# Attention: the V products of a head pair in three groups of four key blocks in place of six groups of two

## The reference, cut to what matters

```
q, k, v = (xn @ w + b)         16 heads of 64, rotary on q and k
scores  = q k^T / 8, masked    1024 x 1024 per head
attn    = softmax(scores)
ctx     = attn @ v
out     = ctx @ o_w + o_b + xn
```

## Time and profile before

| | us |
|---|---|
| runs of the kernel | 2549.84, 2547.35, 2551.39; median 2549.84 |
| the profiled execution's own time | 2540.03 |
| its span (first to last instruction) | 2538.2 |
| granted TensorE clock, mean over the span | 0.923 of full speed |

### The profile page before, as it was taken

How to read it: one execution, slowest core, us unless ns; L and a number is a source line. 1 busy time by engine, 2 the same in 40 slices (tenths; PEclk the granted TensorE clock), 3 DMA queues, 4 the chain that set the end, 5 groups by cost and what they waited for, 6 DMA issues and landing times.

```text
span 2538.2 us, 41109 instructions
## 1 busy us (share of the span) xinstructions
PE 2080.7 (82%) x10326; PEld 1351.3 (53%) x10326; DVE 1746.0 (69%) x3011; ACT 1431.7 (56%) x2785; POOL 902.7 (36%) x733
## 2 busy tenths in 40 slices
PE   3749999879675999987966699997896579999699
PEld 1236666647324666655732466664562256666466
DVE  3957676759485767667947667675794766767588
ACT  3516666647542766655744366664674356666366
POOL 1544242223154433313315534240332453333122
PEclk9879999989896999998979799999897879999889
DMA  2000000001000000001100000000100000000011
GB/s 59 1 25 6 9 8 0 1 25 40 11 0 25 10 5 8 0 1 32 35 10 0 25 10 5 8 0 9 29 29 9 17 13 5 9 4 0 9 35 31
DMA packets 36211, 35.48 MB, mean 14 GB/s; under 512 B 3993, under 2 KB 30977, under 8 KB 36097
## 3 DMA queue, kind: packets, MB, share of 16 engines
q1 hardware_dynamic: 36096, 34.14, 4.6%
HBM read 32.03 MB, written 2.10 MB: 13 GB/s over the span
## 4 chain that ended last, share of the span: by engine, by line
PE 54%; DVE 21%; issue 11%; ACT 8%; POOL 4%; DVEq 1%; ACTq 1%; DMA 0%; SPq 0%; POOLq 0%
PE ps L1314 10%; PE ps L1153 8%; PE ps L1155 6%; PE ps L1154 6%; DVE state L900 5%; PE ps L1303 5%; PE ps L1293 3%; ACT probs L665 3%; DVE turned L948 3%; PE ps L1329 3%; PE ps L1294 3%; PE ps L1421 2%; PE ps L1181 2%; ACT probsT L677 2%; DVE q_split L963 2%
## 5 line engine op out<-in xcount | busy, mean ns | idle before, releaser
L677 ACT ACTIVATE probsT<-ps 128x512 f32<-128x512 f32 (+3 forms) x768 | 351.1, 498 | 446.3 <-PE ps L1303 445.0
L516 POOL TENSOR_TENSOR roped<-turned 128x512 f32<-128x512 f32 x128 | 192.8, 1507 | 663.1 <-DVE turned L948 663.1
L665 ACT ACTIVATE probs<-ps,least 128x640 f32<-128x640 f32 (+7 forms) x512 | 383.3, 749 | 59.5 <-DVE least L973 53.5
L1293 PE MATMUL ps<-k_high,q_split 128*128 128x512 f32 (+3 forms) x768 | 310.0, 404 | 65.4 <-POOL k_low L527 38.7
L1303 PE MATMUL ps<-ident,probs 128*128 128x128 f32 x2304 | 349.9, 279 | 10.3 <-ACT probsT L677 10.1
L1303 PEld LDWEIGHTS ps<-ident,probs 128*128 128x128 f32 x2304 | 261.5, 142 | 133.8 <-issue 94.3
L1314 PE MATMUL ps<-probsT,vals 128*64 128x512 f32 (+3 forms) x1536 | 293.0, 506 | 5.2 <-ACT probsT L677 5.2
L973 DVE CUSTOM_DVE_ANT_0 ps<-ps,row_masks 128x128 f32<-128x128 f32 (+3 forms) x256 | 127.6, 498 | 222.7 <-PE ps L1294 220.2
L980 DVE TENSOR_REDUCE least<-ps 128x1 f32<-128x640 f32 (+3 forms) x256 | 262.3, 1024 | 8.8
L1294 PE MATMUL ps<-k_low,q_split 128*128 128x512 f32 (+3 forms) x768 | 260.6, 352 | 0.0
L725 ACT ACTIVATE hid<-ps,cols 128x512 f32<-128x512 f32 x256 | 176.5, 690 | 103.1 <-PE ps L1155 76.6
(11 more groups left out here) (213 smaller groups left out, 4135.6 us busy)
## 6 DMA issues: line engine op xcount, KB each, us to landing
w<-in_w SPq DMA_DIRECT2D x128, 128.0 KB, 2.0
w_pair<-in_w_pairs SPq DMA_DIRECT2D x36, 256.0 KB, 2.7
xin<-in_x SPq DMA_DIRECT2D x5, 512.0 KB, 3.9
out<-acc SPq DMA_DIRECT2D x4, 512.0 KB, 3.6
pos<-in_c_pos SPq DMA_DIRECT2D x1, 512.0 KB, 4.9
v_w<-in_v_w SPq DMA_DIRECT2D x1, 512.0 KB
o_w<-in_o_w SPq DMA_DIRECT2D x1, 512.0 KB
v_b<-in_v_b SPq DMA_DIRECT2D x1, 512.0 KB
```

What stands on the lines that cost most here:

```text
L516: pool.tensor_tensor(roped[:, k, c * HALF:(c + 1) * HALF], turned[:, 0, g % 2, :], turned[:, 1, g % 2, :], ALU.add).then_inc(roped_ready, 1)
L665: act.activation(probs[:, t % 2, 0:width(t)], banks(2 * (t % 2))[:, 0:width(t)], ACT.Exp, bias=least[:, t:t + 1], scale=-1.0, accum_out=ro ...
L677: act.activation(dst, ps[:, T_BANK + g % 2, 0:k1 - k0], ACT.Copy).then_inc(t_taken, 1)
L1293: pe.matmul(o, q, k_high[par][h][:, k0:k1], start=True, stop=False)
```

## The change

Three groups replace six. Half 1 of the pair before is made in slots 2 (key blocks 0 to 3) and 5 (key blocks 4 to 7); half 0 of this pair is made in slot 11 (key blocks 0 to 3). The products, their operands and the order among them are the same. No wait is added or taken away, and no other engine's code is touched.

```
-                        if t in (1, 3, 5, 7) and not first:
-                            weigh_values(n - 1, 1 - par, 1, (t - 1, t))
-                        if t in (10, 11):
-                            weigh_values(n, par, 0, (2 * t - 20, 2 * t - 19))
+                        if t in (2, 5) and not first:
+                            weigh_values(n - 1, 1 - par, 1, tuple(range(TPH)) if t == 2 else tuple(range(TPH, TILES)))
+                        if t == 11:
+                            weigh_values(n, par, 0, tuple(range(TPH)))
```

## The result

| | before | after |
|---|---|---|
| median of 4 runs each on the same chip, us | 2548.6 | 2610.17 |
| ratio to before, 95% interval | 1 | 1.024 (1.0223 to 1.0258) |
| the profiled execution's own time, us | 2540.03 | 2611.41 |
| its span, us | 2538.2 | 2609.6 |
| granted TensorE clock, mean | 0.923 | 0.915 |

The account below looks back on a forecast made before the run. PE was taken to bound slots 1 to 6, DVE slots 7 to 10, then PE and ACT alternating. 1.09 + 1.38 = 2.47 us, times 24 = 59.3, plus 4.8, on 2549.8 gave 2614 us; range 2580 to 2634.

Parts of the forecast that it names:

- The joins: Merging groups of V products saves 0.14 us per join; merged groups take 3.58, 2.31 and 2.31 us.
- the rival by which the joins pay (2537): All V products: 88 joins save 0.14 us each, 12 us in all, and nothing waits; 2537 us, chance 0.07.
- Slots 1 to 6: Loop pair until project(7): bare slots shrink less than filled ones grow, +1.09 us in sum.
- fixed floor: Slots without V products: none shorter than about 1.92 us, as project must wait until DVE's `turned` empties the one bank.
- Slots 10 and 11: Loop pair: values(1) starts 0.13 us earlier, V products behind it take 1.51 more; transposes come 1.38 us later.
- slot 7 gives nothing back: Slot 7 is 0.80 us lighter on PE, but DVE sets that stretch, so +1.09 us stays.
- a rival for all pairs behind the two waits (2729): Slot 11: the clock falls behind waits of 1.32 and 1.5 us, +115 us more, 2729 us; chance 0.05.
- a clock below 1.00 in a loop pair: Changed profile, any loop pair: a granted clock under 1.00 would show the working wrong.
- the rival of 2581: DVE's stretch: its copy escapes POOL, 0.43 us for 2.27, so a pair costs only +1.09; 2581 us, chance 0.13.
- Pair 0: First pair of each batch: slot 11 +1.51, slot 10 -0.3, so +1.2 us, times 4 = +4.8 us.
- Pair 7: Last pair of each batch: shift hidden behind a 2.42 us wait, 0 us, bounds -0.5 and +1.5 each.
- my likeliest range: Whole kernel: 2.0 to 3.0 us per loop pair with the ends of pairs 0 and 7, 2596 to 2630 us.

Follow-up runs that it names:

- the experiment in slot 10: Half 0 as one group in slot 10 behind the output product, half 1 as before, against the kernel before: 2537.81 us, 0.9966.
- Half 1 alone: Only half 1 moved to slots 2 and 5, half 0 as before, against the kernel before: 2595.27 us, 1.0192; again 2593.39 us.
- Half 0 alone: Only half 0 moved to slot 11 as one group, half 1 as before, against the kernel before: 2580.55 us, 1.0142.
- half 0 ahead: Half 0 as one group in slot 10 ahead of the output product, half 1 as before, against the kernel before: 2523.99 us, 0.9907.

## Why the prediction was right

The order of the steps is that of the working.

- **The joins.** 3.58, 2.31 and 2.31 us, to the hundredth. But a join is worth more than its own 0.14: with what stands beside it, 0.23 in the window of the experiment in slot 10 and 0.33 in the period. In the changed kernel PE has 0.41 us less to do in a pair, and waits for more than that, so the rival by which the joins pay (2537) falls. That the 0.14 comes from the change between 64 and 128 columns is not shown: no run has a join without it.
- **Slots 1 to 6.** +1.03 measured, +1.09 said. Slot 1 1.92 (said 1.92), slot 2 4.99 (5.05), slot 3 1.70 (1.80), slot 4 2.02 (1.91), slots 5 and 6 5.84 (5.85). A slot without V products lasts from project's start until the bank is free, as said, and PE waits 0.55, 0.28 and 0.36 us at the ends of slots 1, 3 and 4. But 1.92 us is no fixed floor: `turned` starts 1.11, 0.89 and 1.21 us behind project in these slots and runs 0.75, which with the 0.06 gives the 1.92, 1.70 and 2.02. Slot 3 lies 0.1 below my lower bound for it, and slot 4 above my value by as much; the two cancel. Half 1 alone shows it apart (+1.0).
- **Slots 10 and 11.** From project(7) to values(1) 12.26 us against 333.47 - 321.08 = 12.39: -0.13 as said. From values(1) to the transposes 3.39 against 1.78: +1.61, said +1.51; the 0.1 is `values` itself, 1.08 behind a wait where it was 0.98. Half 0 alone gives +1.52 for the period. The kernel with half 0 ahead shows from the other side that the loss is the place behind the wait: the same group there gains.
- **What I overlooked.** Slot 7's lighter work goes into slot 10's wait: 2.06 us in place of 1.32. I had said that slot 7 gives nothing back, and did not draw the wait that follows from it. In itself it costs nothing, since DVE sets that stretch; but it is the wait behind which the clock fell.
- **The clock.** Here the working was wrong and got away with it. I gave the lower clock 0.05, as a rival for all pairs behind the two waits (2729), and named a clock below 1.00 in a loop pair as a sign that I am wrong. That sign came in 13 of 24 pairs, behind the first wait and not the second. In 12 of them it slowed only slot 10's products, and the new wait in slot 11 took that up; in one it reached slot 11 and cost 2.0 us. Nothing in my working had this, so the small cost is luck. At 1.6 us each, as with half 1 alone, the 13 would have added 19 us more: 2629, still in the range.
- **DVE's copy.** 2.27 us as before; the rival of 2581 falls.
- **Pair 0** +1.16 from slot 0 to slot 14 in three batches, +0.42 in the first, said +1.2. **Pair 7** +0.33 in three batches and -0.2 in the first, said 0. Its V products of slot 5 run at the lower clock again, as said, 4.05 us for the sixteen.
- **The sum.** For the profiled executions: 24 x 2.52 + 2.0 (clock) + 3.9 + 0.8 = 67.2 of the 71.4 us between the spans; said 64.1. The other 4.2 are outside the pairs: the part ahead of the first pair is 4.4 us longer, where a transfer landed later (6.95 us in place of 6.09) and products ran at the lower clock (L1181 7.60 in place of 5.42), the part between two batches' attention about 0.5 longer, and the end is 1.6 shorter. I had no term for these. The medians differ by 61.6, ten less than the two profiled executions: before, the profiled one lay 8.6 us below the median, after, 1.2 above. So the 2614 is 4 above what was measured, and part of that closeness is luck too. The upper end of my likeliest range was added up wrong: 24 x 3.0 + 6 + 6 gives 2634 and not 2630.

## What to carry to other kernels

A group of products is worth most directly ahead of a wait that another engine sets, and costs its full length directly behind one. Here 0.80 of the 2.31 us stood behind the wait to begin with: all of it ahead made a loop pair 0.9 us shorter, all of it behind 1.5 us longer. Where one PSUM bank is handed back and forth in each slot, filler has to be in every slot: a slot without it lasts as long as the hand-over, and what it would have hidden there is paid in full in another slot. Count a wait that grows without lying on the path, too: the products behind it can come out at the lower clock. Whether that costs anything is decided by the next wait behind them. Read the granted clock itself and not only the lengths, or a fall that a wait has hidden is missed, and comes due when that wait is removed.

## What the runs showed of the hardware

- Behind waits of 1.92 to 2.06 us in slot 10 the granted clock went to its lower level (1.2 GHz) in 13, 16 or 22 of 24 pairs, by the kernel, and in the same pairs in a second execution of two of them; behind waits of up to 1.4 us in slot 10 never. A fall cost 1.6 us where no wait stood behind it. Where one of 1.50 us did, it cost nothing in 12 of 13 pairs, and 2.0 in the one where the lower clock lasted into slot 11. The Trainium skill, TensorE: Matmul & The Clock Gate, section What's actually happening, has the lower level follow idleness; that it follows a wait as short as this, in some pairs and not in others of the same order, I had not expected.
- DVE's copy to `inverse_wide` (128x512, 0.43 us alone) and its L963 (64x1024, 1.22 us alone) don't run beside POOL's `k_low`: whichever starts first holds the other up. In the kept traces all 300 copies that began inside a `k_low` ended 0.28 or 0.29 us behind its end, after 0.79 to 2.29 us; an L963 begun inside one ended 1.07 to 1.08 us behind it; and a `k_low` begun inside an L963 took 3.09 us in place of 2.36. `add_output` (L1000) is not held: it takes its 0.68 us inside the second `k_low` of the pair as elsewhere.
- From a batch's last output product to the first of the next batch's pair 0 it is 319.1 us before and 324.0 with half 1 in groups of one; and in one and the same kernel, half 0 ahead, 323.2, 319.6 and 323.5 from batch to batch. Where it is longer, more of its products stand at the lower clock; that this is the whole of it is not shown. A gain of a few us inside the attention can be lost there.
